# A graph attention layer: GpSimd multiplies the gathered values between its own gathers

## What is computed

```python
q = (feats @ Wq + bq).reshape(n, H, D)
k = (feats @ Wk + bk).reshape(n, H, D)
v = (feats @ Wv + bv).reshape(n, H, D)
score = jnp.sum(k[src] * q[dst], axis=-1)
score = jnp.exp(jnp.clip(score / SCALE, -5.0, 5.0))
wv = jax.ops.segment_sum(v[src] * score[..., None], dst, num_segments=n)
z = jax.ops.segment_sum(score, dst, num_segments=n)
wv = wv / (z[..., None] + 1.0)
```

## Time and profile before

| | |
|---|---|
| median of 3 timed runs | 2921.49 us |
| their range | 2921.08 to 2924.81 us |
| span of the profiled execution | 3375.5 us |
| own time of the profiled execution | none is given beside the span |
| first gather loop in the profile | 161 to 1531 us |
| second gather loop in the profile | 1602 to 2888 us |

### The profile page before, as it was taken

How to read it: one execution, slowest core, us unless ns; L and a number is a source line. 1 busy time by engine, 2 the same in 40 slices (tenths; PEclk the granted TensorE clock), 3 DMA queues, 4 the chain that set the end, 5 groups by cost and what they waited for, 6 DMA issues and landing times.

```text
span 3375.5 us, 29216 instructions
## 1 busy us (share of the span) xinstructions
PE 1462.2 (43%) x4582; PEld 639.7 (19%) x4583; DVE 2090.7 (62%) x3685; ACT 1242.7 (37%) x3273; POOL 1809.4 (54%) x1818
## 2 busy tenths in 40 slices
PE   3133444455434343334233344442323322477996
PEld 2011111111111111013011111110101100376553
DVE  5745567667645555666466677885655656743456
ACT  0022233333323332343255556554444445421122
POOL 3476666666666666660666666666666666111011
PEclk9995666666656655666555555555555555568986
DMA  5321222222222222220111122221111111116410
GB/s 126 76 50 47 50 49 51 49 50 49 53 49 54 51 47 53 53 54 16 39 47 49 49 51 51 59 53 47 49 41 47 47 24 24 37 60 206 135 66 6
DMA packets 124348, 186.68 MB, mean 55 GB/s; under 512 B 62045, under 2 KB 79154, under 8 KB 124127
## 3 DMA queue, kind: packets, MB, share of 16 engines
q0 software_dynamic: 57776, 89.59, 12.6%
q1 hardware_dynamic: 48894, 70.70, 6.8%
q10 hardware_dynamic: 17618, 25.71, 2.1%
HBM read 146.04 MB, written 39.84 MB: 55 GB/s over the span
## 4 chain that ended last, share of the span: by engine, by line
issue 25%; DVE 24%; PE 19%; DVEq 13%; ACT 10%; another core or an unknown queue 6%; ACTq 2%; POOL 1%; DMA 0%; POOLq 0%
ACT arena L1255 6%; PE mm L838 4%; DVE arena L1863 4%; PE mm L696 4%; DVE red L1877 3%; DVE red L1976 3%; PE hist L916 2%; PE l L987 2%; PE hist L778 2%; DVEq L1754 2%; DVEq L1876 2%; PE l L756 2%; DVE score L1843 2%; PE l L916 1%
## 5 line engine op out<-in xcount | busy, mean ns | idle before, releaser
L558 POOL DMA_INDIRECT arena<-b_tab,lin x815 | 813.7, 998 | 559.8 <-issue 344.3
L558 POOL DMA_INDIRECT arena<-kv_tab,rec x815 | 824.4, 1012 | 334.5 <-issue 299.1
L756 PE MATMUL l<-arena,identB 128*128 128x512 bf16 x996 | 395.1, 560 | 502.0 <-issue 265.1
L1255 ACT ACTIVATE arena<-arena,lin 128x64 f32<-128x64 f32 x1984 | 504.3, 334 | 213.0 <-issue 213.0
L838 PE MATMUL mm<-Wslots,eaT 48*128 48x512 f32 x248 | 234.2, 1097 | 684.5 <-ACT eaT L1249 320.3
L1976 DVE TENSOR_REDUCE red<-arena 128x128 f32<-128x2048 f32 x189 | 459.2, 2486 | 13.7 <-issue 12.8
L1863 DVE TENSOR_SCALAR arena<-arena,digit 128x512 bf16<-128x512 int16 x744 | 257.2, 414 | 97.4 <-issue 49.8
L756 PEld LDWEIGHTS l<-arena,identB 128*128 128x128 bf16 x996 | 115.3, 127 | 771.1 <-issue 456.0
L778 PE MATMUL hist<-arena,oh_lo 125*128 125x225 bf16 x400 | 170.7, 584 | 175.0 <-DVE arena L1834 142.8
L838 PEld LDWEIGHTS mm<-Wslots,eaT 48*128 48x128 f32 x248 | 72.2, 321 | 775.4 <-ACT eaT L1249 331.0
L1252 ACT ACTIVATE arena<-arena 128x1024 f32<-128x1024 f32 x62 | 65.5, 1057 | 394.0 <-DVE arena L1999 277.3
(11 more groups left out here) (380 smaller groups left out, 2445.5 us busy)
## 6 DMA issues: line engine op xcount, KB each, us to landing
arena<-at_tab SPq DMA_DIRECT2D x50, 800.0 KB, 4.5
at_tab<-T ACTq DMA_DIRECT2D x25, 800.0 KB
arena<-kv_tab,rec POOLq DMA_INDIRECT x815
arena<-b_tab,lin POOLq DMA_INDIRECT x815
at_pack<-arena SPq DMA_DIRECT2D x25, 256.0 KB
T<-at_pack SPq DMA_DIRECT2D x25, 256.0 KB
lin_tab<-lin ACTq DMA_DIRECT2D x62, 64.0 KB
lin<-lin_tab SPq DMA_DIRECT2D x62, 56.0 KB
```

The costliest lines, as they stand in the source:

```text
L558: return pool.indirect_dma_start(dst, None, table, offs(ap=index, axis=0))
L756: last = pe.matmul(l3[:, 0, :], identB[:], hot[:, j], start=False, stop=True, skip_group_check=True)
L1255: last = act.activation(dst[:, s], hh[u][:, s, 0:C], ACT.Identity, bias=bias[:, s:s + 1])
```

## The change

POOL gets a function, `weigh_values`, which multiplies the gathered values by the weights for one step. In step g it is issued before slot 9, and handles step g-1 in the other buffer; one call more stands behind the loop. It waits for `weights_ready`, which DVE now gives inside its one-hot loop, after the first 8 one-hot rows, where it also masks the exponentials (L1870 before). The next step of POOL waits for `weighted_ready` ahead of its gathers. DVE drops L1872, releases `G[u]` behind the one-hot rows, and at the end of step g sums and adds the weighted values of step g-1 (`add_weighted`); one call more stands behind the loop. Ahead of the loop DVE clears `weighted[1]`.

```diff
--- before.py
+++ after.py
@@ -329,6 +329,7 @@
         dst_final, dst_out = sem("dst_final"), sem("dst_out")
         w_spread, w_diag = sem("w_spread"), sem("w_diag")
         score_ready, exp_ready = sem("score_ready"), sem("exp_ready")
+        weights_ready, weighted_ready = sem("weights_ready"), sem("weighted_ready")
 
         class Gather:
 
@@ -603,7 +604,15 @@
                 pool.wait_ge(stage_out[k], 16 * len(PAIRS[k::NSTAGE]))
             pool.wait_ge(rec_out, 32)
 
-            def gather_loop(L, buf, table):
+            def weigh_values(g, u):
+
+                pool.wait_ge(weights_ready, g + 1)
+                pool.tensor_tensor(weighted[u][:, :, 0:C].rearrange("p s (h c) -> p s h c", h=HEADS),
+                                   G[u][:, :, C:2 * C].rearrange("p s (h c) -> p s h c", h=HEADS),
+                                   weighted[u][:, :, C:C + HEADS].unsqueeze(3).to_broadcast([P, SLOTS, HEADS, HD]),
+                                   ALU.mult).then_inc(weighted_ready, 1)
+
+            def gather_loop(L, buf, table, weigh=False):
 
                 pairs = pool.value_load(totI[0:1, 0:1], min_val=HI + 1, max_val=STEPS // 2 - 8)
                 pool.wait_ge(L.win_ready, 1)
@@ -614,8 +623,12 @@
                         left = word & 31
                         pool.wait_ge(L.rec_landed[u], 16 * (i + 1))
                         pool.wait_ge(L.free, 2 * i + u + 1)
+                        if weigh:
+                            pool.wait_ge(weighted_ready, 2 * i + u + 1)
                         pool.sem_inc(pool_steps, 1)
                         for s in range(SLOTS):
+                            if weigh and s == SLOTS // 2 + 1:
+                                weigh_values(2 * i + u, 1 - u)
                             if s == SLOTS // 2:
                                 pool.wait_ge(L.win_ready, 2 * i + u + 2)
                                 pool.wait_ge(L.rec_used, 2 * i + u + 1)
@@ -625,12 +638,14 @@
 
                             with (pool.If(left >= s + 1) if s else nullcontext()):
                                 gather(buf[u][:, s], table, rec[u][:, s, 0:1]).then_inc(L.rows_landed[u], 16)
+                if weigh:
+                    weigh_values(2 * pairs, 1)
                 pool.wait_ge(L.rec_landed[0], 16 * (pairs + 1))
                 pool.sem_inc(pool_steps, 1)
 
             pool.wait_ge(steps_in, 16)
             pool.wait_ge(codes_out, 16)
-            gather_loop(LOOP0, G, kv_tab)
+            gather_loop(LOOP0, G, kv_tab, weigh=True)
             pool.wait_ge(b_out, 16 * len(PAIRS))
             pairs = pool.value_load(totI[0:1, 0:1], min_val=HI + 1, max_val=STEPS // 2 - 8)
             with aligned(pool, 0, pairs) as i:
@@ -1810,6 +1825,9 @@
 
 
             dve.wait_ge(steps_in, 16)
+            dve.memset(weighted[1], 0.0)
+            d().then_inc(weighted_ready, 1)
+            d().then_inc(weights_ready, 1)
             begin_loop(LOOP0)
             dve.memset(accV, 0.0)
             for k in range(NSTAGE):
@@ -1832,6 +1850,14 @@
                 cols = bass.ds(t, 8)
                 tt(oh_lo[:, u], lane_of[n], bm(partB[:, cols], P), ALU.is_equal)
                 tt(oh_hi[n][u], code_of[n], bm(codeB[:, cols], NB * R), ALU.is_equal).then_inc(hist_oh, 1)
+
+            def add_weighted(g, u):
+                dve.wait_ge(weighted_ready, g + 2)
+                red_(red[:, 0:C + HEADS], weighted[u].rearrange("p s c -> p c s"), X_AXIS, ALU.add)
+                d()
+                v_ = accV[:, bass.ds(block_in(before), 1), :]
+                tt(v_, v_, red[:, 0:C + HEADS].unsqueeze(1), ALU.add)
+                d()
 
             def step0(i, u, with_hist):
                 blk = step_head(LOOP0, i, u)
@@ -1863,22 +1889,15 @@
                         last = ts(onehot[:, (u + q) % 2, j], colI, G[u][:, s, 2 * C:2 * C + 1], digit[u][:, s:s + 1],
                                   op0=ALU.is_equal, op1=ALU.mult)
                     last.then_inc(oh_ready, 1)
+                    if q == 1:
+                        dve.wait_ge(exp_ready, 2 * i + u + 1)
+                        tt(weighted[u][:, :, C:C + HEADS], expd[u][:], bc(masks[u], HEADS), ALU.mult).then_inc(
+                            weights_ready, 1)
+                d().then_inc(LOOP0.free, 1)
                 if with_hist:
                     type_hots(0, 2 * i + u, 8 * (2 * i + u), u)
-                dve.wait_ge(exp_ready, 2 * i + u + 1)
-                e_ = weighted[u][:, :, C:C + HEADS]
-                tt(e_, expd[u][:], bc(masks[u], HEADS), ALU.mult)
-                d()
-                tt(weighted[u][:, :, 0:C].rearrange("p s (h c) -> p s h c", h=HEADS),
-                   G[u][:, :, C:2 * C].rearrange("p s (h c) -> p s h c", h=HEADS),
-                   e_.unsqueeze(3).to_broadcast([P, SLOTS, HEADS, HD]), ALU.mult)
+                add_weighted(2 * i + u, 1 - u)
                 end_step(u)
-                d().then_inc(LOOP0.free, 1)
-                red_(red[:, 0:C + HEADS], weighted[u].rearrange("p s c -> p c s"), X_AXIS, ALU.add)
-                d()
-                v_ = accV[:, bass.ds(blk, 1), :]
-                tt(v_, v_, red[:, 0:C + HEADS].unsqueeze(1), ALU.add)
-                d()
 
             pairs = dve.value_load(totI[0:1, 0:1], min_val=HI + 1, max_val=STEPS // 2 - 8)
             with aligned(dve, 0, HI) as i:
@@ -1887,6 +1906,7 @@
             with aligned(dve, HI, pairs) as i:
                 for u in range(2):
                     step0(i, u, False)
+            add_weighted(2 * pairs, 1)
             dve.wait_ge(LOOP0.rec_landed[0], 16 * (pairs + 1))
             dve.wait_ge(at_full, NB + 1)
             dve.wait_ge(at_out, 16 * (NB + 1))
```

## The result

The changed kernel takes 3035.1 us (median of 4 runs, 3032.39 to 3037.84) against 2922.72 us of the kernel before beside it (4 runs, 2921.08 to 2924.81). The ratio is 1.038 [1.0368, 1.0393], so the change costs 112 us. The forecast was 3068 us, in a range of 3025 to 3150.

The account below looks back on a forecast made before the run. The prediction took POOL's queue of gathers and fetches to bound the first loop in timed runs. Product 155, clearing 1 and DVE's relief -10 sum to +146 us on 2921.5 us: 3068 us, range 3025 to 3150.

Parts of the forecast that it names:

- The pace of the timed run: Both gather loops: without the profile's pauses, timed runs go nearly at POOL's pace, the first loop about 1180 us.
- The argument of the 454 us: Profiled execution took 454 us longer than the timed median; POOL's losses in the two loops make 425 of it.
- The product, 62 x 2.5 = 155 us: First loop: each of 62 steps gives POOL a product of 2.5 us in its queue, bounds 1.2 and 5.5.
- The test that the prediction set: Product's slot on POOL, gather start before to gather start after, less 1.31 us, should be near 2.5 us.
- The waits: POOL's waits in the first loop: weights ready 8.5 us into a step, wanted at 13; `weighted_ready` costs nothing.
- DVE's relief, -10 us: First loop: DVE's shorter step gives back 10 us, only in the 24 steps with few slots where DVE sets the pace.
- The earlier release: Releasing `G[u]` earlier in DVE's step saves nothing, as POOL wants the buffer only a whole step later.
- Start and end: Around the first loop: clearing `weighted[1]` costs 1 us; the last addition, 1.2 us later, hides behind L1918's wait.
- Contention makes the product dear: Rival, first loop: DVE's passes hold each product to 3.3 to 4.9 us, +196 to +295 us; dearer product 15 in 100.
- DVE is the bound: Rival, every first-loop step: DVE sets the timed pace too, so the change gives -68 us, 2853 us; 5 in 100.
- The balance: Rival, first loop: half the pauses remain, +81 us, 3003 us; 8 in 100, shared with a product of 1.2 to 2.0 us.
- no change: Rival, first loop: the change does nothing, needing 2.5 us free on POOL in each step; 2 in 100.

Follow-up runs that it names:

- e1: The kernel before, unchanged, timed and profiled again on a chip without pauses: 2926.87 against 2925.21 us, ratio 1.0006.
- e4: The kernel before without DVE's product (L1872 and its drain left out, zeros summed instead), on a chip without pauses: 2905.21 us, ratio 0.9933.
- e12: The changed kernel with a second POOL product over 15 of 16 slots, into a buffer nothing reads, on a chip without pauses: 3151.66 us, ratio 1.078.
- e8: The changed kernel, unchanged, on the chip that pauses: 3339.71 us, ratio 0.9899 against the kernel before.
- e9: The changed kernel with POOL's product cut to one slot of 16, all waits kept, on a chip without pauses: 2937.07 us, ratio 1.0044.
- e3: The changed kernel with the product back on DVE, keeping the new order and the late sum, on a chip without pauses: 2941.89 us, ratio 1.0054.
- e7: The changed kernel with POOL's product ahead of slot 4 instead of slot 9, on the chip that pauses: 3512.9 us, ratio 1.0218.
- e5: The changed kernel with POOL multiplying slots 0 to 7 and DVE slots 8 to 15, on the chip that pauses: 3411.8 us, ratio 0.993.
- e6: The changed kernel with DVE making the product too, into a buffer nothing reads, on the chip that pauses: 3393.98 us, ratio 0.9861.
- e11: The changed kernel with DVE making the product too, into a buffer nothing reads, on a chip without pauses: 3046.03 us, ratio 1.0414.
- e2: The changed kernel with a second POOL product over 15 of 16 slots, on the chip that pauses: 3414.02 us, ratio 0.9931.

## Why the prediction was right

**The pace of the timed run: right in what the change met, wrong in where it comes from.** The reading that the pauses don't belong to the runs that are timed, and that POOL sets the pace in them, is shown by e1 (1152.1 us for a floor of 1150; the 1180 that was given for the whole loop was 28 too long), by e4 (81 us off DVE give 20) and by e12 (111 us onto POOL make its loop 112 longer). The sentence that failed is that the pauses "belong to the profiled execution alone". They belong to a chip, or to a condition of it: on the pausing chip the timed runs have them too, with times as long as the profiled spans, and there the sign is the other one (e8). Had the runs that were to be predicted been of that kind, the forecast would have missed by 6%; that they were not was, in part, luck. The argument of the 454 us showed that the timed runs had no such pauses; it did not show that no timed run has them.

**The product, 62 x 2.5 = 155 us: the step that was mis-sized.** It takes 1956 ns and not 2.5 us. With the gaps (-7.6 us) it cost 121.3 - 7.6 = 113.7 us, or 1.83 a step, 41 us less than said. The mean of the two one-input passes was too dear by a quarter. The test that the prediction set, from the start of the gather before to that of the gather after less 1.31, gives 1008.34 - 1004.55 - 1.31 = 2.48 us in the step shown and 2.37 in the mean, and would have confirmed 2.5; it misleads, since the gather of 1.66 us before the product is long for DVE's work beside it, as other gathers were before (e9 has the same 1.66 with a product of 0.31). The second test, that the time moves by no less than 62 such slots less 10 us, gives 62 x 2.37 - 10 = 137 us against 112 measured, and would have called the reading wrong for the same reason. The loop's own sum is what decides. The Trainium skill's figure for 2048 elements (GPSIMD Engine Reference, section 3.1), halved to an estimate of 2.3 us, was nearer than the rows' 2.5 and still above the 1.96 measured.

**The gathers, +5.9 us: in no term.** They come with the new order and not with the product, as e3 and e9 have them without it (+8.1 and +9.9).

**The waits: right.** The mask was to be ready 4 us before POOL wants it; it is 4.1 to 5.0 us. (The parts that the prediction names, 1.4 + 3.5 + 3.1 + 0.2, make 8.2 us and not 8.5.) That the cover matters is shown by e7. `weighted_ready` holds nobody (2.0 us of idle time at the sum, 1.3 of it issue).

**DVE's relief, -10 us: right**, with -8.1 us of POOL's waits (the rest of the 9.7 is mostly the first gather's wait for its records, 1.3 us, which is no relief). It came about as said: the six waits that went lie in the steps of few slots, and e4, in which DVE's step only gets shorter, has none of them either. In e4 the gathers also got 12.6 us shorter. In the changed kernel they didn't, and the order is the likely reason.

**The earlier release: nothing, as said, on a quick chip**; e3 keeps both waits of e1. On the pausing chip POOL's waits for the release are 25.7 us in the profile of before and 1.2 to 1.8 us in e5, e6 and e8. Whether the earlier release does this is not shown, as the order alone was not run there.

**Start and end.** The start is 2.3 us later and not 1. The end was to be hidden behind L1918's wait, and it is: the reciprocal behind that line begins 20.4 us after the last gather in e1 and 19.1 after. The stretch from the last gather to the second loop is still 2.2 us longer; it varies from 86.3 to 93.7 us among the kernels of the quick chips, and what sets it was not looked for.

By terms: 113.7 + 5.9 - 9.7 + 2.3 + 2.2 is 114.4, against a prediction of 155 - 10 + 1 + 0 = 146. The forecast was 33 us above the result, and the product alone is 41 us less than said. The result was inside the range, but by the prediction's own cases it was an unlikely one: 3035.1 us lies just below the 3037 to 3111 that had 70 in 100, and a product under 2.0 us belonged to the case with 8.

**The rivals.** *Contention makes the product dear* falls here: 1956 ns in the mean, and no product of the first loop over 2.0 us. It falls because the product meets the sum, as was argued; e11 shows the contention when something else is there, and it is DVE that pays in nearly all steps. *DVE is the bound* falls on the quick chip by e4 and e11, and comes true in sign on the pausing one, at -1.0% instead of -2.3%. Its mechanism is neither shown nor excluded there: with DVE's product put back the ratio keeps the gain (e6), and the profiled loop loses most of it. *The balance* and *no change* fall. The 1% on the pausing chip goes with fewer pauses of DVE in the first loop; why they become fewer, and what makes that chip pause, stays open.

**What the profile was to show.** Products of 2.2 to 2.8 us: no, 1.96. First loop longer by less than in the timed runs: not so, as the profile after is of a quick chip (+109.7 us against e1, and shorter than rows 2). POOL's waits before fetches: 138.7 to 69.0 us between pausing profiles, and no change between quick ones (27.1 and 28.7), where there were none. DVE's waits for rows: yes, 264.3 us.

## What to carry to other kernels

Before work is moved from one engine to another, compare the span of the profile with the timed runs: where they differ, find which engine sets the pace without the difference, and price the move there; here the profile's slack on POOL (200 us) was no slack in the time. Then ask whether the timed runs themselves are all of one kind, since the same change cost 3.8% on one chip and gave 1.0% on another. And a wait placed behind several queued instructions costs nothing until it is moved ahead of them (e7: 3.5 us a step), so the place of a moved step in its new queue is worth as much thought as its length.

## What the runs showed of the hardware that was not expected

- One chip pauses. Register and branch instructions in the queues of DVE, POOL and SP take some 0.7 us there in bursts (347, 129 and 30 of them of 0.6 us or more in the first profile of before; none in e1), those of ACT and PE next to never. In the first loop DVE's pauses are all but gone where DVE waits for POOL (1 in e7, 8 in e2, 133 in the profile of before). The kernel before takes 3373 to 3437 us with them and 2925 without. Its arithmetic has the same lengths: the multiplication of 128x1024 takes 1225 ns on both.
- POOL's product of two inputs, the second one broadcast: 312 ns for 64 elements a partition, 1065 for 512, 1850 for 960, 1956 for 1024. That is about 1.7 ns an element and 0.2 us.
- POOL's gap of 0.30 us after a gather is not there when arithmetic follows, and is 0.16 us when a gather follows arithmetic; between two products there is none.
- A DVE instruction with two inputs that overlaps POOL's product mostly ends after it, although it started first by the records (L1851 in e11, 0.69 us become 3.08), while DVE's sum beside the product loses next to nothing (2.13 us against 2.10). One-hot rows are drawn out too: in e7, where the product falls on them, they take 326.9 us in the loop against 253.6 in the changed kernel.
- A gather takes 0.944 us in the median, and longer at some places where DVE passes from one long instruction to the next: 1.13 us from L1872 to the sum and 1.30 from L1834 to L1872 in e1, 1.71 from L1852 to the sum in the changed kernel (means of some 50 gathers each).
